# Spline attention: VectorE's gate and clip in pieces between dependent passes, a running minimum, and key tiles of 128

## The reference

```
sim  = einsum('bhnd,bhdm->bhnm', q, k) / sqrt(32)
xs   = clip(nan_to_num(sim), -6, 6)
kan  = base_w * silu(xs) + einsum('...k,k->...', b_splines(xs), coef)   # cubic splines, 8 bases
attn = softmax(kan, axis=-1)
out  = Wo @ einsum('bhnm,bhmd->bhnd', attn, v)
```

## Time and profile before

| | |
|---|---|
| three runs | 7359.88, 7373.56, 7383.81 us, median 7373.56 |
| profiled execution | 7378.02 us, span 7376.0 us, mean granted clock 0.971 |
| busy over the span | PE 6612.3 us (90%), VectorE (DVE) 6213.3 (84%), ScalarE (ACT) 5765.7 (78%), GpSimd (POOL) 5396.8 (73%) |
| spline pipeline | from 1966.84 us (first scores) to the end |

### The profile page before, as it was taken

How to read it: one execution, slowest core, us unless ns; L and a number is a source line. 1 busy time by engine, 2 the same in 40 slices (tenths; PEclk the granted TensorE clock), 3 DMA queues, 4 the chain that set the end, 5 groups by cost and what they waited for, 6 DMA issues and landing times. The chain is left out here.

```text
span 7376.0 us, 141185 instructions
## 1 busy us (share of the span) xinstructions
PE 6612.3 (90%) x40618; PEld 4490.3 (61%) x40618; DVE 6213.3 (84%) x9509; ACT 5765.7 (78%) x9040; POOL 5396.8 (73%) x3374
## 2 busy tenths in 40 slices
PE   6777889999699999999999999999999999999998
PEld 4655547677366666666666666666666666666666
DVE  4333665454499999999999999999999999999997
ACT  5445113333399999999999999999999999999997
POOL 4334000000299999999999999999999999999997
PEclk7888999999799999999999999999999999999998
DMA  2000000000200000000000000000000000000000
GB/s 73 21 19 26 1 0 0 0 0 0 63 11 1 1 1 1 1 1 11 1 1 1 1 1 1 11 19 1 1 1 1 1 2 2 4 4 4 4 4 6
DMA packets 75949, 56.14 MB, mean 8 GB/s; under 512 B 50776, under 2 KB 73464, under 8 KB 75032
## 3 DMA queue, kind: packets, MB, share of 16 engines
q1 hardware_dynamic: 72512, 53.88, 2.6%
q10 hardware_dynamic: 3288, 0.33, 0.0%
HBM read 37.80 MB, written 16.37 MB: 7 GB/s over the span
## 5 line engine op out<-in xcount | busy, mean ns | idle before, releaser
L1552 POOL TENSOR_TENSOR a_s<-a_s,a_v 128x784 f32<-128x784 f32 x1568 | 2912.6, 1858 | 306.1 <-ACT a_s L1763 287.6
L1588 PE MATMUL a_right_sides<-a_s,diag_d 128*128 128x392 f32 x6272 | 2284.5, 507 | 8.4 <-POOL a_s L1552 1.0
L1588 PEld LDWEIGHTS a_right_sides<-a_s,diag_d 128*128 128x128 f32 x6272 | 1132.1, 190 | 1052.4 <-POOL a_s L1552 309.3
L1684 DVE SCALAR_TENSOR_TENSOR a_kan<-a_s,spline_c,a_kan 128x784 f32<-128x784 f32 x1568 | 1621.4, 1034 | 50.7 <-issue 0.3
L1611 PEld LDWEIGHTS a_weighed<-a_V,a_probT 112*128 112x128 f32 x10976 | 1375.5, 193 | 162.2
L1545 POOL TENSOR_TENSOR a_inner<-a_inner,a_x 128x784 f32<-128x784 f32 x784 | 1459.0, 1861 | 0.0
L1611 PE MATMUL a_weighed<-a_V,a_probT 112*128 112x65 f32 x10976 | 1366.3, 270 | 0.0
L1763 ACT ACTIVATE a_s<-a_v 128x784 f32<-128x784 f32 x1568 | 1335.3, 852 | 4.6
L1754 ACT ACTIVATE a_v<-a_a 128x784 f32<-128x784 f32 x1568 | 1336.0, 852 | 0.3
L1600 PE MATMUL a_turned<-ident,a_prob 128*112 128x128 f32 x5488 | 856.6, 278 | 229.8 <-ACT a_probT L1770 228.5
L1655 DVE TENSOR_SCALAR a_x<-a_scores 128x392 f32<-128x392 f32 x1568 | 874.6, 558 | 19.9 <-PE a_scores L1575 19.9
(11 more groups left out here) (196 smaller groups left out, 5814.3 us busy)
## 6 DMA issues: line engine op xcount, KB each, us to landing
rows<-bias_rows_dram SPq DMA_DIRECT2D x112, 91.0 KB
X<-in_x_dram SPq DMA_DIRECT2D x4, 1568.0 KB, 13.5
a_q<-q_dram SPq DMA_DIRECT2D x392, 16.0 KB, 2.0
mask<-in_window_mask_dram SPq DMA_DIRECT2D x56, 98.0 KB
v_dram<-V SPq DMA_DIRECT2D x14, 227.5 KB, 2.3
a_V<-v_dram SPq DMA_DIRECT2D x4, 796.2 KB, 8.8
q_dram<-Q SPq DMA_DIRECT2D x14, 224.0 KB, 1.9
k_dram<-K SPq DMA_DIRECT2D x14, 224.0 KB, 1.9
```

Source lines behind the costliest of these rows:

```text
L1552: eng.tensor_tensor(s, s, v, ALU.mult).then_inc(cubed, 1)
L1588: mm = eng.matmul(up[:, j, 0:SUB], steps[i][:, :], cubes[g][:, SUB * j:SUB * (j + 1)], start=(i == 0), stop=(i == 1))
L1684: eng.scalar_tensor_tensor(F, banked((s1, s2)[j][g][:, :]), c[:, 3 + j:4 + j], F, ALU.mult, ALU.add).then_inc(left_added, 1)
```

## The change

Four edits, in the spline attention alone.

1. VectorE's order. The gate moves to the start of the step (of the same group as before: three steps back now, in the step after), in two halves of 392 columns, one bank each, the second behind add_tanh. The second clip half becomes two pieces of 196 columns. Every pass that depends on the one before has a piece between. invert and add_output stand between the first gate half and add_tanh.
2. The row's extremum. add_right writes the negated sum and keeps a running minimum: the minimum of group g - 1 is the accumulator's starting value, read as a per-partition scalar. row_max and negated_max are gone; exponent uses scale -1 and the last minimum as bias.
3. The keys. 24 tiles of 128 and one that overlaps its neighbour (its first 64 keys have zero values and zero ones), in seven chunks of 4, 4, 4, 4, 2, 4, 3 tiles. Values are projected, stored and loaded in that form.
4. Semaphore counts follow (two right_gated per group).

```diff
+TURNED3 = (0, 4, 8, 12, 16, 18, 22, KEY_TILES3)          # KEY_TILES3 = 25
+def tiles3(ch): return range(4 * ch, min(4 * ch + 4, KEY_TILES3))
+def turned3(ch): return range(TURNED3[ch], TURNED3[ch + 1])
+def first_key3(k): return min(P * k, L - P)
...
 def turn(ch):
-    last = min(4 * TILE * (ch + 1) - 1, L - 1) // QUART
+    last = (min(P * TURNED3[ch + 1], L) - 1) // QUART
...
-        for j in range(4):
-            at = TILE * (4 * ch + j)
-            mm = eng.transpose(tp[:, j, :], prob[r][:, at:at + TILE], m.ident[:, :])
+        for j, k in enumerate(turned3(ch)):
+            at = first_key3(k)
+            mm = eng.transpose(tp[:, j, :], prob[r][:, at:at + P], m.ident[:, :])
...
-def gate(g):
+def gate(g, j):
+        at = slice(SUB * j, SUB * (j + 1))                # SUB = 392
         eng.wait_ge(right_made, 4 * t + g + 5)
         eng.wait_ge(turned, 7 * t + min(2 * g + 2, 7))
-        eng.scalar_tensor_tensor(banked(part(r, g)), banked(x[g][:, :]), 0.0, U, ALU.is_gt, ALU.mult).then_inc(right_gated, 1)
+        eng.scalar_tensor_tensor(part(r, g)[:, at], x[g][:, at], 0.0, up[:, j, 0:SUB], ALU.is_gt, ALU.mult).then_inc(right_gated, 1)
 def clip(g, j):
-        eng.tensor_scalar(x[g][:, SUB * j:SUB * (j + 1)], scp[:, j, 0:SUB], 6.0, -6.0, ALU.min, ALU.max).then_inc(clipped, 1)
+        first, end = ((0, SUB), (SUB, SUB + SUB // 2), (SUB + SUB // 2, 2 * SUB))[j]
...
+        if j != 1:
+            ins.then_inc(clipped, 1)
 def add_right(g):
-        eng.wait_ge(right_gated, n + 2)
+        eng.wait_ge(right_gated, 2 * n + 4)
         eng.wait_ge(left_added, 2 * n + 10)
+        if g == 3:
+            eng.wait_ge(exp_done, 4 * t + 4)
+        eng.wait_ge(all_added, n + 1)
         eng.sem_inc(waits_met_v, 1)
-        eng.tensor_tensor_reduce(out=f, in0=F, in1=f, scale=1.0, scalar=-3.0e38, op0=ALU.add, op1=ALU.max,
-                                 accum_out=gmax[r][:, g:g + 1]).then_inc(all_added, 1)
+        eng.tensor_tensor_reduce(out=f, in0=F, in1=f, scale=-1.0, scalar=gmin[r][:, g - 1:g] if g else 3.0e38, op0=ALU.add, op1=ALU.min,
+                                 accum_out=gmin[r][:, g:g + 1]).then_inc(all_added, 1)
...
-    order += [(add_tanh(g3), l3)] + between[0] + [(times_x(g3), l3)] + between[1] + [(left(g3, 0), l3), (clip(g, 0), 0), (left(g3, 1), l3),
-              (clip(g, 1), 0), (add_right(g3), l3), (gate(g2), l2)]
+    small = {1: [(invert, 3)], 2: [(add_output, 4)]}.get(g, [])
+    order += [(gate(g3, 0), l3)] + small + [(add_tanh(g3), l3), (gate(g3, 1), l3), (times_x(g3), l3), (clip(g, 0), 0), (left(g3, 0), l3),
+              (clip(g, 1), 0), (left(g3, 1), l3), (clip(g, 2), 0), (add_right(g3), l3)]
...
 def exponent(g):
-        eng.wait_ge(max_ready, t + 1)
-        eng.activation(part(r, g), part(r, g), ACT.Exp, bias=nmax[r][:, :]).then_inc(exp_done, 1)
+        eng.wait_ge(all_added, 4 * t + 5)
+        eng.activation(part(r, g), part(r, g), ACT.Exp, scale=-1.0, bias=gmin[r][:, 3:4]).then_inc(exp_done, 1)
```

More of the change, by code:

```diff
@@ L1292, with tiles3, turned3, first_key3 @@
 BLOCKS3 = PAIRS3 * TILES3
+TAIL3 = L % P
+KEY_TILES3 = L // P + 1
+CHUNKS3 = -(-KEY_TILES3 // 4)
+TURNED3 = (0, 4, 8, 12, 16, 18, 22, KEY_TILES3)
+def tiles3(ch):
+    return range(4 * ch, min(4 * ch + 4, KEY_TILES3))
+def turned3(ch):
+    return range(TURNED3[ch], TURNED3[ch + 1])
+def first_key3(k):
+    return min(P * k, L - P)
 def pipeline_pairs(eng, stages):
@@ L1333, in attention3 @@
         k.k_dram = [dram(f"k3_dram{b}", (P, L)) for b in range(B)]
-        k.v_dram = [dram(f"v3_dram{b}", (TILE, TILES, 2 * V1)) for b in range(B)]
+        k.v_dram = [dram(f"v3_dram{b}", (P, KEY_TILES3, 2 * V1)) for b in range(B)]
         spline_constants3(nc, m, k)
@@ L1432, in _ @@
                     else:
-                        for q in range(4):
-                            at = TILE * (4 * k + q)
+                        for q, tile in enumerate(tiles3(k)):
+                            at = first_key3(tile)
                             for i in range(HALVES):
-                                mm = pe.matmul(bank[0:TILE, P * q:P * (q + 1)], xn[:, i, at:at + TILE], m.WT[:, W_V3 + i, :],
+                                mm = pe.matmul(bank[:, P * q:P * (q + 1)], xn[:, i, at:at + P], m.WT[:, W_V3 + i, :],
                                                start=(i == 0), stop=(i == 1))
@@ L1460, in kan_attention3 @@
         inner = [sb(f"inner{g}", [P, QUART]) for g in range(2)]
-        gmax = [sb(f"gmax{r}", [P, 4]) for r in range(2)]
-        rmax = [sb(f"rmax{r}", [P, 1]) for r in range(2)]
-        nmax = [sb(f"nmax{r}", [P, 1]) for r in range(2)]
+        gmin = [sb(f"gmin{r}", [P, 4]) for r in range(2)]
         rinv = sb("rinv", [P, 1])
@@ L1469, in kan_attention3 @@
         fp = ps("kan", [P, 2, 512])
-        tp = ps("turned", [TILE, 4, P])
+        tp = ps("turned", [P, 4, P])
         op = ps("weighed", [P, V1])
@@ L1608, in stage @@
                         eng.wait_ge(copied, 7 * t + ch + 2)
-                        for j in range(4):
-                            k = 4 * ch + j
-                            mm = eng.matmul(op[:, :], probT[(r + ch) % 2][:, j, :], V[p % 2][:, k, :], start=(k == 0), stop=(k == TILES - 1))
+                        for j, k in enumerate(turned3(ch)):
+                            mm = eng.matmul(op[:, :], probT[(r + ch) % 2][:, j, :], V[p % 2][:, k, :], start=(k == 0), stop=(k == KEY_TILES3 - 1))
                         mm.then_inc(weighed, 1)
@@ L1617, in project_out @@
                     eng.wait_ge(x_added, t + 4)
[L1618 removed]
+                    eng.wait_ge(right_gated, 8 * t + 32 if not isinstance(t, int) else min(8 * t + 32, 8 * BLOCKS3 + 2))
                     rows = slice(VW * (p % 2), VW * (p % 2 + 1))
@@ L1723, in _ @@
                 for g in range(4):
-                    (g2, l2), (g3, l3) = (((g - back) % 4, int(g < back)) for back in (2, 3))
-                    between = {1: ([(invert, 3)], []), 2: ([], [(add_output, 4)]), 3: ([(row_max, 1)], [(negated_max, 1)])}.get(g, ([], []))
-                    order += [(add_tanh(g3), l3)] + between[0] + [(times_x(g3), l3)] + between[1] + [(left(g3, 0), l3), (clip(g, 0), 0), (left(g3, 1), l3),
-                              (clip(g, 1), 0), (add_right(g3), l3), (gate(g2), l2)]
+                    g3, l3 = (g - 3) % 4, int(g < 3)
+                    small = {1: [(invert, 3)], 2: [(add_output, 4)]}.get(g, [])
+                    order += [(gate(g3, 0), l3)] + small + [(add_tanh(g3), l3), (gate(g3, 1), l3), (times_x(g3), l3), (clip(g, 0), 0), (left(g3, 0), l3),
+                              (clip(g, 1), 0), (left(g3, 1), l3), (clip(g, 2), 0), (add_right(g3), l3)]
                 pipeline_pairs(dve, order)
```

45 lines of the change are left out of this document (24 added, 21 removed).

## The result

The changed kernel takes 7393.41 us (median of 10 runs, 7390.99 to 7398.01) against 7372.66 us of the kernel before in the same comparison (10 runs): a ratio of 1.003, interval 1.0022 to 1.0039. It is slower by 21 us; about 50 were forecast. The profiled execution has a span of 7391.9 us against 7376.0, 15.9 more.

The account below looks back on a forecast made before the run. VectorE was taken to pace the kernel; its own sum gained nothing, but late scores made steps of 6.89, 7.06, 6.92 and 6.70, 27.57 us a block, +0.25 x 196 = +48 us: 7424 us, 8-in-10 range 7310 to 7490.

Parts of the forecast that it names:

- the step 1 to 2: From group 1's first clip to group 2's: scores wait for tanh, copy, transposes and fold_heads, 7.06 us against VectorE's own 6.96.
- VectorE alone: VectorE's own instructions in a block of the spline attention: about 27.3 us against 27.32, so no gain by itself.
- The rival without a chain: Slack in PE's transposes or the copy leaves only VectorE's sum: 27.31 us a block, no change, 7378 us; chance 0.23.
- Unfilled gaps: The fillers don't fill VectorE's gaps, 0.32 us a group stays: 28.59 us a block, +249 us, 7627; chance 0.03.
- Rival 2: VectorE is the only bound, waits and pointer reads run ahead during fillers: 26.87 us a block, -88 us, 7290; chance 0.19.
- 2 to 3: From group 2's first clip to group 3's: the chain to the scores, with a two-tile chunk's transposes, sets 6.92 us.
- 0 to 1: From group 0's first clip to group 1's: no copy in the chain, VectorE sets 6.89 us, with invert and pointer.
- 3 to 0: From group 3's first clip to the next group 0's: chain below VectorE's own time, which sets 6.70 us.
- The pieces: VectorE's extra instructions: gate in two halves +0.06 us, second clip half in two pieces of 196 columns +0.07, per group.
- add_right's queue: On VectorE, add_right's satisfied wait behind the last clip piece: 0.06 us a group, bounds 0 and 0.18.
- the pointer's 0.065: On VectorE, add_right reads the running minimum as pointer scalar: +0.065 us, three times a block, bounds 0 and 0.07.
- What costs nothing: Items priced at zero: 25 tiles, later second gate half, earlier exponent bias, invert's cover, loads; value projection a microsecond or two.

Follow-up runs that it names:

- experiment 3: The changed kernel with the two-tile chunk of keys moved from chunk 4 to chunk 2: 7388.09 us (a single run).
- experiment 2: The changed kernel with the old 28 key tiles of 112 in chunks of four, keeping VectorE's new order and the running minimum: 7477.98 us, ratio 1.0135.
- experiment 4: The changed kernel with the gate in pieces of 196, 196 and 392 columns and the clip in two halves around the first left: 7440.47 us, ratio 1.0085.
- experiment 7: The changed kernel with fold_heads, keep_o and project_out on partitions 0 to 63 for every pair: 7368.80 us (a single run).
- experiment 1: The kernel before with only the 25 key tiles in seven chunks; VectorE's order, gate and maximum as before: 7359.29 us against 7379.27, ratio 0.9975.
- experiment 8: The changed kernel with an immediate as add_right's start value in every group instead of the running minimum: 7384.08 us (a single run).
- the fastest kernel: The changed kernel with the clip in two halves behind the lefts again and one small reduction of four minima replacing pointers: 7314.80 us, ratio 0.9917.

## Why the prediction was right in its mechanism and wrong in its sum

- **The steady blocks** came as forecast. The scores become late in the step 1 to 2, 7.07 for 7.06. +0.25 a block was said and 0.21 measured, 40.7 us for 48. Part of that closeness is luck. VectorE alone is cheaper than its sum: its steps without a wait, 6.80, 6.93 (experiment 3), 6.74 and 6.67, add up to 27.14, where 27.31 was forecast. The turns of the loop, which no term had, take nearly as much back: 0.21 and 0.08 in every other block, 0.14 a block. The rival without a chain fell (7378; experiments 2, 3 and 4 move the chain and the steps follow). What it had for it, PE issuing while ScalarE still ends, the trace of the kernel before does not show for the transposes: those that the copy releases start 0.05 after its end or later. Unfilled gaps (7627) fell too: every filled pass starts on its filler's heels, times_x 0.47 after the half gate. Rival 2 (26.87 a block) was reached by no kernel: queue and pointer are real, and the scores come late.
- **2 to 3** was 6.92 for all and is 6.74 in even, 6.95 in odd pairs. The earlier trace rows were read in an odd pair, in which ScalarE's passes around keep_o start later (experiment 7); an even one would have shown it, since in the kernel before, too, tanh to copy takes 1.97 in odd and 1.62 in even pairs. **0 to 1** was 6.89 and is 6.80, 6.88 in the first block of each loop turn; invert adds 0.08 there and not 0.13. Its cover held by 0.11 us; where it fails it costs 0.26 a block (experiment 2) and not 0.1. **3 to 0** was 6.70 and is 6.67 or 6.88, the latter again at a loop turn.
- **The pieces** cost what starts said, 0.47 a half gate and 0.27 a short clip. **add_right's queue** was 0.06 and is 0.04 to 0.05 (0.31 or 0.32 behind the piece against 0.27), less than the 0.18 of the earlier trace rows; the pointer's 0.065 is 0.06, 1034 against 974 ns. Mean times by shape, changed kernel:

```profile
L1726 DVE CUSTOM_DVE_ANT_0 a_prob<-a_kan,a_prob,a_gmin 128x784 f32<-128x784 f32 x328 | 339.1, 1034 | 0.0
...
L1726 DVE CUSTOM_DVE_ANT_0 a_prob<-a_kan,a_prob 128x784 f32<-128x784 f32 x109 | 106.2, 974 | 0.0
```

- **The step that failed** is "What costs nothing", in all that lies outside the steady blocks. It put the value projection at "a microsecond or two, on neither side", said of the 25 tiles that PE and ScalarE are not the bound, and gave head and drain no term. That holds for the steady blocks only. Outside them PE's time counts, at a granted clock under 1: projection -4.4, head -6.1, drain -10.0, together -20.5, nearly half of the 48. With this term the forecast is 48 - 20 = 28 us, against 21 by the medians. The three stages, in us, with the granted clock in brackets:

| kernel | key tiles | gate | projection | head | drain |
|---|---|---|---|---|---|
| before | 28 | old | 94.94 (0.86) | 89.02 (0.85) | 43.05 (0.51) |
| tiles alone (experiment 1) | 25 | old | 90.48 (0.88) | 86.57 (0.88) | 33.20 (0.68) |
| order alone (experiment 2) | 28 | new | 95.25 (0.86) | 83.40 (0.92) | 28.01 (0.95) |
| after | 25 | new | 90.49 (0.88) | 82.97 (0.90) | 33.05 (0.68) |
| partitions 0 to 63 (experiment 7) | 25 | new | 90.28 (0.88) | 82.96 (0.90) | 27.18 (0.89) |
| immediate (experiment 8) | 25 | new | 90.95 (0.88) | 82.77 (0.90) | 26.82 (0.90) |

The projection's part goes with the tiles and the head's mostly with the gate's new place. The drain's part, the largest, goes with the clock: 28 tiles took 28.0 us at 0.95, and the changed kernel, at 0.68, took 6 us more than experiments 7 and 8 at 0.89 and 0.90, with the same tiles and order.
- Open: why the clock falls 42 us before the end in the kernel before, 21 in the changed one and 3 to 6 in experiments 2, 7 and 8. No edit is shown to cause it, and each kernel has one profile. Experiment 1 was 20 us faster by the medians, of which projection and head explain 7, so its drain is probably shorter in most executions.

## What to carry to other kernels

A pass moved into a gap has two ends: ask of the filler not only whether it fits, but how much longer its own result is spread out, since here the clip's two ends moved 1.0 us apart and the loop through tanh, copy and transposes had 0.8 of slack. Price the head, the drain and the stage before by their own bound, even where the steady loop pays nothing: a few us each came to half of the loop's effect. And look at the place that a moved pass leaves: an independent pass between two dependent ones may be covering a gap there unseen.

## What the hardware showed unexpectedly

- With keep_o on partitions 0 to 63, keep_o, the magnitude pass and the copy behind it each start 0.07 to 0.10 before the pass ahead of them ends. With keep_o on 64 to 127, in the odd pairs of the changed kernel, the same three start 0.02 or 0.03 after that end (experiment 7): 0.35 us more from tanh to copy (1.97 against 1.62), and 0.21 in the step 2 to 3 of the odd pairs.
- At the start of a loop turn of the changed kernel PE's scores start 0.23 after the matmul before them ends, with only issue ahead of them; in the other blocks they start 0.07 before it ends. The first clip of g = 0 waits 0.2 there; in the kernel before, the gap is 0.14 and the scores are done 1.0 ahead of the clip. That a kernel without loop turns would save it wasn't tried.
- In the profiled execution of the fastest kernel (7329.08 us, against the median of 7314.80) the granted clock dips 15 times between 2190 and 6570 us, to 0.50 for 3.4 us each time, and the gate waits 1.1 us for right sides each time, 17 us in all. Busy times of a stretch without a dip and of the next one, which holds one (columns as above):

```profile
3000.00:3007.50 7.50, 5.96 (x35) 3.98 (x36) 7.46 (x14) 7.43 (x12) 6.78 (x5) 1.00 0.00 0
3007.50:3014.00 6.50, 6.50 (x29) 3.54 (x28) 5.38 (x11) 5.61 (x9) 6.42 (x5) 0.74 0.00 0
```
